# Two groups at a time on TensorE in the first cross attention of a two-layer perceiver block

## The reference

```python
q = (tgt @ Wq.T).reshape(b, t, H, HD).transpose(0, 2, 1, 3)      # tgt: layer-normed x, 2 x 256 rows
k = (src @ Wk.T).reshape(b, s, H, HD).transpose(0, 2, 1, 3)      # src: the context, 2 x 4096 rows
v = (src @ Wv.T).reshape(b, s, H, HD).transpose(0, 2, 1, 3)
scores = jnp.einsum('bhtd,bhsd->bhts', q, k) / np.sqrt(HD)
scores = jnp.where(attention_mask[:, None, None, :], scores, -jnp.inf)
attn = jax.nn.softmax(scores, axis=-1)
out = jnp.einsum('bhts,bhsd->bhtd', attn, v)
```

## Time and profile before

| | |
|---|---|
| median of 3 runs | 1817.34 us (1812.93 to 1818.72) |
| profiled execution | 1811.63 us, of which the recorded span is 1809.9 us |
| the stage of the first cross attention | about 475.6 to 840.2 us of the span |
| PE busy in the whole span | 1580.1 us (87%) |
| DVE, ACT, POOL busy | 1163.3 (64%), 867.6 (48%), 684.6 us (38%) |

### The profile page before, as it was taken

How to read it: one execution, slowest core, us unless ns; L and a number is a source line. 1 busy time by engine, 2 the same in 40 slices (tenths; PEclk the granted TensorE clock), 3 DMA queues, 4 the chain that set the end, 5 groups by cost and what they waited for, 6 DMA issues and landing times. The chain is left out here.

```text
span 1809.9 us, 42047 instructions
## 1 busy us (share of the span) xinstructions
PE 1580.1 (87%) x15948; PEld 891.9 (49%) x15948; DVE 1163.3 (64%) x1757; ACT 867.6 (48%) x1162; POOL 684.6 (38%) x525
## 2 busy tenths in 40 slices
PE   3999999999499999997775958999999999966772
PEld 1455545554133333334342425777777777752432
DVE  4665656565599999993328647666666666335356
ACT  2555555555177777774220014555555555512330
POOL 2340000000111111111423007999999999917100
PEclk9999999999599999998777978999999999978786
DMA  4697888878332222220300047565556555021000
GB/s 164 193 217 239 208 233 212 239 210 213 108 95 64 67 64 69 63 64 9 143 1 1 1 122 223 137 162 149 148 134 164 147 150 130 11 83 38 2 0 12
DMA packets 178219, 212.19 MB, mean 117 GB/s; under 512 B 57096, under 2 KB 151572, under 8 KB 173486
## 3 DMA queue, kind: packets, MB, share of 16 engines
q1 hardware_dynamic: 177520, 210.45, 42.6%
q10 hardware_dynamic: 576, 0.00, 0.0%
HBM read 122.78 MB, written 87.57 MB: 116 GB/s over the span
## 5 line engine op out<-in xcount | busy, mean ns | idle before, releaser
L1121 POOL TENSOR_TENSOR x_r<-x_p 128x1024 f16<-128x1024 f32 x256 | 479.3, 1895 | 23.3 <-ACT x_p L1097 16.6
L1136 DVE TENSOR_REDUCE x_mx<-a_all 128x2 f32<-128x1024 f32 x249 | 304.9, 1225 | 147.3 <-PE a_all L1020 147.3
L1097 ACT ACTIVATE x_p<-s_all 128x1024 f32<-128x1024 f32 x256 | 248.4, 1022 | 222.7 <-PE s_all L1003 222.7
L702 ACT ACTIVATE x_p<-s_all 128x1024 f32<-128x1024 f32 x256 | 261.0, 1023 | 48.7 <-PE s_all L612 41.4
L757 DVE TENSOR_REDUCE x_mx<-a_all 128x1 f32<-128x512 f32 x352 | 229.8, 683 | 15.8 <-PE o_all L623 8.7
L1003 PE MATMUL s_all<-x_q,x_k 64*128 64x256 f16 x3072 | 209.5, 269 | 0.0
L1038 PEld LDWEIGHTS o_all<-x_v,x_p 128*128 128x128 bf16 x2048 | 178.7, 97 | 40.2 <-issue 40.1
L1038 PE MATMUL o_all<-x_v,x_p 128*128 128x129 f16 x2048 | 197.5, 221 | 0.9 <-POOL x_r L1121 0.9
L1039 PE MATMUL o_all<-x_v,x_r 128*128 128x65 f16 x2048 | 192.7, 193 | 0.0
L1039 PEld LDWEIGHTS o_all<-x_v,x_r 128*128 128x128 f16 x2048 | 180.7, 98 | 0.0
L1003 PEld LDWEIGHTS s_all<-x_q,x_k 64*128 64x128 f16 x3072 | 149.1, 94 | 61.9 <-issue 0.6
(11 more groups left out here) (343 smaller groups left out, 2829.3 us busy)
## 6 DMA issues: line engine op xcount, KB each, us to landing
values<-vst SPq DMA_DIRECT2D x16, 2064.0 KB, 10.2
x_v<-values SPq DMA_DIRECT2D x32, 1032.0 KB, 5.3
keys<-kst SPq DMA_DIRECT2D x32, 1024.0 KB, 6.6
x_k<-keys SPq DMA_DIRECT2D x128, 256.0 KB, 5.2
x_k<-keys SPq DMA_DIRECT2D x192, 64.0 KB, 2.1
values<-vst SPq DMA_DIRECT2D x16, 528.0 KB, 11.8
x_v<-values SPq DMA_DIRECT2D x32, 264.0 KB, 2.6
cf<-in_ctxT SPq DMA_DIRECT2D x16, 512.0 KB, 9.4
```

What stands on the lines that cost most here:

```text
L702: act.activation(prob[g % NP][:], chip.s_ps[g % 2][:].rearrange("p (c q) -> p c q", q=SQ), ACT.Exp, scale=hd ** -0.5).then_inc(p_ready, 1)
L1097: act.activation(prob[g % NP][:], chip.s_ps[g % 2][:].rearrange("p (c q) -> p c q", q=SQ), ACT.Exp, scale=hd ** -0.5).then_inc(p_ready, 1)
L1121: pool.tensor_tensor(rest[g % NP][:], prob[g % NP][:], hi, ALU.subtract).then_inc(rest_done, 1)
L1136: dve.tensor_reduce(mx[a[1] % 2][:, n // 4, 2 * (n % 4):2 * (n % 4) + 2], chunk_banks(u, g)[:, :].rearrange("p (h c) -> p h c", h=2), AX.X ...
```

## The change

Three things are written differently, all in `cross_attention_small`. PE takes its steps in twos: for g = 0, 2, 4, 6 it issues the turning and the two chunks of step g, the scores of groups g+2 and g+3, the two chunks of step g+1, the values of groups g-4 and g-3, and last, for g = 4, the folding. VL is 4, so the values of a unit run one group later than before. On ACT `copied` stands behind the exponential of g = 5 and `queries` behind that of g = 6.

```diff
-    GR, GK, W, VL, NP = 8, 4, 4, 3, 8
+    GR, GK, W, VL, NP = 8, 4, 4, 4, 8
...
                 def body(u):
-                    for g in range(GR):
-                        if real(u) or (u[1] == -1 and g >= 6):
-                            s = u if g + 2 < GR else ahead(u, 1)
-                            if s:
-                                scores(s, (g + 2) % GR)
+                    for g in range(0, GR, 2):
                         for place, kind, a, n in body_work(u, g):
                             wait_free(pe, u, place)
                             if kind == "c":
                                 chunk(u, place, a, n)
-                            elif kind == "t":
+                            else:
                                 negated_maxima(u, place, a)
-                            else:
+                        s = u if g + 2 < GR else ahead(u, 1)
+                        if s and (real(u) or (u[1] == -1 and g == 6)):
+                            scores(s, (g + 2) % GR)
+                            scores(s, (g + 3) % GR)
+                        for place, kind, a, n in body_work(u, g + 1):
+                            if kind == "c":
+                                wait_free(pe, u, place)
+                                chunk(u, place, a, n)
+                        if real(u):
+                            for v in (g - VL, g - VL + 1):
+                                if v >= 0:
+                                    values(u, v)
+                                elif not is_first(u):
+                                    values((u[0], u[1] - 1) if u[1] else (u[0] - 1, W - 1), GR + v)
+                        for place, kind, a, n in body_work(u, g + 1):
+                            if kind == "x":
+                                wait_free(pe, u, place)
                                 folded(u, place, a)
-                        if real(u):
-                            if g >= VL:
-                                values(u, g - VL)
-                            elif not is_first(u):
-                                values((u[0], u[1] - 1) if u[1] else (u[0] - 1, W - 1), GR + g - VL)
...
-                        if g == 4 and ahead(u, -1):
+                        if g == 5 and ahead(u, -1):
                             copied(ahead(u, -1))
-                        if g == 5 and ahead(u, 1):
+                        if g == 6 and ahead(u, 1):
                             queries(ahead(u, 1), 8)
```

## The result

| | before | after |
|---|---|---|
| median | 1815.21 us (4 runs) | 1854.16 us (4 runs, 1849.56 to 1858.01) |
| ratio, 95% interval | | 1.0212 [1.0179, 1.0245] |
| profiled execution, span | 1811.63, 1809.9 us | 1856.16, 1854.4 us |
| first cross attention, first chunk to last output | 475.6 to 840.4: 365 us | 478.1 to 884.4: 406 us |

The change makes the kernel 39 us slower, inside the range, 2 us under the forecast. In the profiles the stage is 41 us longer (forecast 41); it begins 2.5 us later in the execution after, and the rest differs by under 1 us.

The account below looks back on a forecast made before the run. DVE was taken to set the pace, waiting 0.47 us a unit. Its work and waits summed to 12.34 us against 10.96, +1.38 a unit; 29 x 1.38 + 0.6 = 40.6, so +41 us, median 1856, range 1844 to 1872.

Parts of the forecast that it names:

- What bounds the kernel: In the stage before the change, DVE sets the pace: 10.49 us of work a unit plus about 0.47 of waiting.
- Step 1: Behind two groups of values and the turning, place 9 comes late, so DVE waits 0.43 us a unit.
- rival D: Groups of values in the loop follow at 0.64 us, not 0.43: +0.5 a unit more, +55 us, 1871; chance 0.07.
- Step 3: Place 11 needs the bank freed by ACT's `queries`, now behind the exponential of group 6: DVE waits 0.97 us a unit.
- Rival A: `queries` is done early enough that place 11 does not starve DVE: +0.41 a unit, +12 us, 1829; chance 0.07.
- Step 4: The folding's result is ready only at 5.81 us, after DVE's chunks end at 5.45: the output waits 0.36 us.
- Step 5: In the next pair of steps the ring of chunk banks runs short before place 0's maximum: DVE waits 0.09 us.
- Sum: All DVE work and waits together: 12.34 us a unit against 10.96, +1.38 a unit over 29 units.
- The first unit: The unit ahead of the 29 full ones has no folding and was forecast to lose about 0.6 us.
- rival C: PE's new pause of some 1.4 us a unit lowers the granted clock: +180 us, about 2000; chance 0.03.
- The cover of the loads: Loads for the unit four ahead start 0.4 us closer to their first reader; existing distance covers that, costing nothing.
- Rival B: PE is the true bound and saved switches feed the ring, removing DVE's waits: -14 us, 1804; chance 0.04.

## Why the prediction was right

- **What bounds the kernel**: DVE, with 0.47 us a unit of waiting. Right, and shown by the run with the later maximum of maxima, which changes DVE's order alone and gains 10 us (7 of them in the stage).
- **Step 1**, the wait behind the turning: 0.43 forecast, 0.41 measured. The unseen distance from values to turning, taken as 0.57, is 0.57 (661.17 to 662.17, less 0.43). The 16 records of two groups take 1.07, which is 0.43 + 0.64, so groups of values follow each other at 0.43 in the loop and rival D falls. Its price was also loosely worked out: its four slips of 0.21 add up to 0.84, the sum used 0.5, and no reason is given.
- **Step 3**, the held chunk: 0.97 forecast, 1.02 measured; it starts 3.87 us after place 7 (3.82 forecast). Undoing the line takes away 23 us of the 39, and 30 once the loads are in time; delaying it further adds 30 at full clock. Shown from both sides. Rival A falls with it.
- **Step 4**, the output: wait 0.36 forecast, 0.43 measured, but the output itself takes 0.44 in place of 0.55, probably since DVE stands empty when it begins; no run tests that. Together 0.87 for 0.91, which is in part luck. That the same working does not give the price of moving the folding was seen later: 2 to 3 us at full clock for the 6 to 7 expected.
- **Step 5**, the ring: 0.09 forecast and seen: the slots from 667.22 end at 669.62, the next maximum starts at 669.71.
- **The unit read above** closes: 10.49 + 0.41 + 1.02 + 0.43 - 0.11 + 0.09 = 12.33, and its two columns on POOL stand 12.33 apart. The units repeat in fours, 12.07 to 12.40 us:

```profile
660.32 0.21 POOL L739 TENSOR_TENSOR x_mcol<-x_nm,x_zero 128x4 f16<-128x4 f32 x1 [10.78 <-DVE x_nm L772]
...
672.65 0.21 POOL L739 TENSOR_TENSOR x_mcol<-x_nm,x_zero 128x4 f16<-128x4 f32 x1 [10.71 <-DVE x_nm L772]
```

- **Sum**: +1.38 us a unit forecast, 12.25 - 10.92 = +1.33 measured, so 38.5 us over the 29 units for 40.0. The first unit made up for it: 0.6 forecast, and the columns of units two and three stand at 499.76 and 513.17, 13.41 apart, where they were 10.94 apart (496.76 and 507.70): +2.5. There the matmuls still ran at half clock, until after the values at 505.08:

```profile
505.08 1.93 PE L652 MATMUL o_all<-x_p,x_vf 128*32 128x256 f32 x16
...
508.78 1.07 PE L652 MATMUL o_all<-x_p,x_vf 128*32 128x256 f32 x16
```

  In the kernel before the clock had risen by 496 us. That the late rise made the 2.5 us is read from these rows and not tested; if so, it is a piece of rival C. The two errors cancel, and that the total came out at 41 is luck to this extent.
- **The cover of the loads** held in the changed kernel (one wait of 0.4 us on PEld in the view of waits), as said. But it held because the unit grew longer: at 11.4 us a unit it was gone, at 6 to 7 us, and at 11.1 in single steps the waits were there as well. I had priced it only for the time that I forecast.
- **Rival B**, a gain from fewer switches: the switches are saved as priced (x16 in 1.07) and nobody waited for them. Rival A's 1829 was met by undoing the copy alone, but by luck: 6 to 7 us of it are the late loads, and without them the kernel stands 9 us over the one before, not 12.
- **Rival C**, the clock: given 0.03. It did not come in this kernel, but it was nearer than that. The same pause of 1.25 us with other work behind it brings the unit above 13 us in 12 of 29 units, and with 2.09 us it is 14.9 us or more in 28 of 29. The count of matmuls per time, by which I set it aside, does not separate them: 2417 in 250 us at clock 1.00 in the change, 2362 at 0.95 with the folding first, which is as much effect as cause.

## What to carry to other kernels

With a ring of buffers shared by several kinds of work, the price of a new order is found by following each buffer to whoever frees it, through the in-order queue of that engine: here a copy that takes 0.38 us was put behind one more exponential and held a chunk, and all of PE behind it, for 1.25 us. Before saving time on an engine, show by one small run that it sets the pace; PE at 49.8 of 50 us busy did not, and the one maximum that DVE took too early did. When a forecast rests on a cover ("the loads are in time"), price it for the other outcomes as well.

## What the runs showed of the hardware that I had not expected

- A pause of PE of 1.25 us once per 12 us can bring the granted clock from 1.00 to 0.50 for over three microseconds, or not, by what stands around it: never from 525 to 875 us with the values directly behind the held chunks (the change), in 12 of 29 units with the folding in between. What decides it is open; no run varied the work behind the pause alone at equal timing. The Trainium skill (TensorE: Matmul & The Clock Gate, Part 1) says that the gate sets the clock by how busy PE has been recently; the falls seen here agree, and its two levels are the two seen.
- Matmuls whose results nobody reads, issued in such a pause, paid here: five of them a unit gave 12 us, fourteen gave 58.
- The maximum of maxima reads the result of the maximum just ahead of it on DVE and starts only after that one's end (659.56 + 0.68 to 660.39). It takes 0.34 us of DVE's slots so, and 0.07 when one other maximum stands between.
